# Attention and expert layer on one core: late weight loads moved to the synchronisation engine's queue, zeroing moved to unit 6, one transfer for a unit's maxima, row-max stream one tile further ahead

## The reference

```python
q = (x @ Wq).reshape(B, T, 16, 16).transpose(0, 2, 1, 3)
k, v = ...                                   # 4 key/value heads, each repeated 4 times
att = einsum('bhqd,bhkd->bhqk', q, k) * scale + alibi + causal
att = softmax(att)
y = einsum('bhqk,bhkd->bhqd', att, v) ... @ Wo
x = layernorm(x + y)
logits = x @ router_w.T                      # 8 experts, top 1, sigmoid of the winning logit
routed = sum over experts of (up * silu(gate)) @ down, rows scaled by the score
shared = silu(x @ shared_gate_w) * (x @ shared_up_w) @ shared_down_w
x = layernorm(x + shared + routed)
```

## Time and profile before

| quantity | value |
|---|---|
| median of 3 runs | 568.99 us (565.54 to 570.54) |
| the profiled execution | 567.3 us |
| its span, first to last instruction | 565.6 us |
| PE busy in the span | 511.2 us, 90% |
| ACT, DVE, POOL busy | 260.4, 299.2, 212.4 us |
| mean granted clock of TensorE | 0.951 |

### The profile page before, as it was taken

How to read it: one execution, slowest core, us unless ns; L and a number is a source line. 1 busy time by engine, 2 the same in 40 slices (tenths; PEclk the granted TensorE clock), 3 DMA queues, 4 the chain that set the end, 5 groups by cost and what they waited for, 6 DMA issues and landing times.

```text
span 565.6 us, 7685 instructions
## 1 busy us (share of the span) xinstructions
PE 511.2 (90%) x2474; PEld 250.9 (44%) x2474; DVE 299.2 (53%) x624; ACT 260.4 (46%) x529; POOL 212.4 (38%) x305
## 2 busy tenths in 40 slices
PE   5876799979999999989987989999989999999991
PEld 2322233323332333321245754664665666656561
DVE  1767799978987888880035734212222333323332
ACT  2634487968897879887920031011013222222310
POOL 4433343634443434331201005870003454554543
PEclk9988599999999999998978889999999999999997
DMA  7669420564554545310233700231112222122210
GB/s 219 121 173 301 121 50 3 129 198 92 170 97 164 96 166 114 146 38 3 82 100 115 235 1 1 76 109 39 56 57 66 66 63 77 57 75 67 61 52 28
DMA packets 39462, 54.91 MB, mean 97 GB/s; under 512 B 5887, under 2 KB 27971, under 8 KB 39316
## 3 DMA queue, kind: packets, MB, share of 16 engines
q1 hardware_dynamic: 29792, 30.93, 21.2%
q0 software_dynamic: 5952, 19.56, 11.1%
q10 hardware_dynamic: 3680, 3.94, 2.1%
HBM read 34.72 MB, written 17.52 MB: 92 GB/s over the span
## 4 chain that ended last, share of the span: by engine, by line
PE 71%; DVE 11%; DMA 7%; ACT 4%; issue 3%; SPq 2%; POOL 1%; POOLq 0%; ACTq 0%; DVEq 0%
PE ps L785 14%; PE ps L705 10%; PE ps L607 9%; PE ps L596 7%; PE ps L804 7%; PE ps L583 7%; DVE mx L971 6%; DMA qk_or_dn<-mrow 5%; PE ps L716 5%; PE ps L553 3%; PE ps L677 3%; PE ps L796 2%; ACT probs L886 2%; PE ps L694 1%; DVE eq L966 1%
## 5 line engine op out<-in xcount | busy, mean ns | idle before, releaser
L886 ACT ACTIVATE probs<-ps 128x512 f32<-128x512 f32 x288 | 155.4, 613 | 33.4 <-PE ps L596 33.0
L971 DVE TENSOR_REDUCE mx<-ps 128x1 f32<-128x512 f32 (+3 forms) x240 | 148.2, 649 | 36.2 <-PE ps L583 35.7
L583 PE MATMUL ps<-qk_or_dn 127*128 127x128 bf16 (+3 forms) x576 | 114.4, 284 | 11.9 <-DVE mx L971 6.5
L596 PE MATMUL ps<-qk_or_dn 127*128 127x512 bf16 x288 | 103.6, 392 | 9.0 <-DMA qk_or_dn<-mrow 6.0
L583 PEld LDWEIGHTS ps<-qk_or_dn 127*128 127x128 bf16 x576 | 47.6, 100 | 92.7 <-DVE mx L971 38.4
L785 PE MATMUL ps<-wgu,tmp 128*128 x184 | 82.9, 593 | 0.1
L607 PE MATMUL ps<-probs,Vs 128*32 128x512 f32 x576 | 78.2, 615 | 0.7 <-ACT probs L886 0.7
L1260 POOL TENSOR_SCALAR_AFFINE_SELECT probs<-probs 128x512 f32<-128x512 f32 x64 | 40.7, 636 | 96.1 <-ACT probs L886 96.0
L1219 POOL TENSOR_SCALAR_AFFINE_SELECT dg<-dg 128x512 f32<-128x512 f32 x64 | 40.8, 638 | 46.2 <-ACT dg L842 46.1
L1318 POOL DMA_INDIRECT rows<-acc,tok x23 | 22.6, 981 | 87.7 <-DMA acc<-x_all 42.3
L596 PEld LDWEIGHTS ps<-qk_or_dn 127*128 127x128 bf16 x288 | 26.6, 98 | 55.1 <-ACT probs L886 33.1
(11 more groups left out here) (118 smaller groups left out, 498.3 us busy)
## 6 DMA issues: line engine op xcount, KB each, us to landing
wgu<-in_gu POOLq DMA_DIRECT2D x8, 1024.0 KB, 5.7
qk_or_dn<-qparts SPq DMA_DIRECT2D x36, 128.0 KB
yT<-yU SPq DMA_DIRECT2D x16, 256.0 KB, 2.0
qk_or_dn<-in_dn SPq DMA_DIRECT2D x8, 512.0 KB, 8.2
tmp<-xs SPq DMA_DIRECT2D x23, 128.5 KB, 2.2
qparts<-wgu SPq DMA_DIRECT2D x6, 384.0 KB, 4.1
tmp<-yT SPq DMA_DIRECT2D x34, 64.0 KB
xs<-rows POOLq DMA_DIRECT2D x1, 2056.0 KB, 12.2
```

The lines of the kernel that those rows point to most:

```text
L583: mm = pe.matmul(ps[:, bank, i * w:(i + 1) * w], Q6[k][0:KROWS, h0 + i, qi * P:(qi + 1) * P], K6[k][0:KROWS, k0:k0 + w], start=True, stop= ...
L596: pe.matmul(o, K6[k][0:KROWS, kb * P:(kb + 1) * P], Q6[k][0:KROWS, :, qi * P:(qi + 1) * P], start=True, stop=True).then_inc(s_st, 1)
L886: act.activation(probs[:, 4 * (s % 3) + p, :], ps[:, 4 + (4 * s + p) % SB, :], ACT.Exp, scale=SCALE).then_inc(s_exp, 1)
L971: dve.tensor_reduce(o, ps[:, a_bank(u, t), 0:nh * w].rearrange("p (h w) -> p h w", h=nh), AX.X, ALU.max).then_inc(s_amax, 1)
```

## The change

Four edits. The six late loads leave ACT's projection jobs; SP issues `x_all` at the end of its unit 0 and the five weight loads at the end of its unit 1 (`load_late`), and for this SP's loop is written out. `zero_slots` goes from slot 4 of unit 1 to slot 4 of unit 6. `max_rows` issues one transfer of 3 partitions instead of three of one, and the waits on `s_mrow` count 16 for a unit instead of 48. `AHEAD` goes from 19 to 20 and `FIRST_AHEAD` from 13 to 14.

```diff
-LEAD, AHEAD, FIRST_AHEAD = 6, 19, 13
+LEAD, AHEAD, FIRST_AHEAD = 6, 20, 14
...
                 sp.wait_ge(s_amax, turn_count(u, last))
-                n = HG * NQ
-                for p in range(3):
-                    sp.dma_start(Q6[i][p:p + 1, :, :].rearrange("o h t -> o (h t)")
-                                 .rearrange("o (a b) -> o a b", a=n),
-                                 mrow[p * n:(p + 1) * n, :]).then_inc(s_mrow, 16)
+                sp.dma_start(Q6[i][0:M_ROWS, :, :].rearrange("p h t -> p (h t)")
+                             .rearrange("p (a b) -> p a b", a=HG * NQ), mrow[:]).then_inc(s_mrow, 16)
...
+            def load_late(dst, src, done):
+                sp.dma_start(dst, src.rearrange("(k p) n -> p k n", p=P)).then_inc(done, 16)
...
-            with sp.Fori(0, LOOPS, 1) as it:
-                for k in range(STEP):
-                    step(it * STEP + k, k)
-            for u in range(LOOPS * STEP, NU):
-                step(u, u % STEP, last=(u == NU - 1), more=False)
+            for u in range(NU):
+                step(u, u % STEP, last=u == NU - 1, more=u + 2 < NU)
+                if u == 0:
+                    load_late(x_all[:], x_d, s_x)
+                if u == 1:
+                    for dst, src in ((wo, wo_d), (rt, rt_d)):
+                        load_late(dst[:], src, s_wo)
+                    for dst, src in ((wsg, sg_d), (wsu, su_d), (wsd, sd_d)):
+                        load_late(dst[:], src, s_wsh)
...
-                i = 2 * (n - LATE_AT)
-                for dst, src, done in later_loads[i:i + 2] if i >= 0 else []:
-                    act.dma_start(dst, src.rearrange("(k p) n -> p k n", p=P)).then_inc(done, 16)
...
-                    if s == 4 and u == 1:
+                    if s == 4 and u == NU - 2:
                         zero_slots()
```

More of the change, by code:

```diff
@@ L42 @@
 STEP = 3
-LOOPS = (NU - 2) // STEP
-assert LOOPS * STEP == NU - 2
 CF_ID, CF_SEL, CF_IOTA, CF_LE, CF_THR = 0, 128, 256, 264, 328
@@ L98 @@
 DIRECT = 4
-FIRST_A, LATE_AT, ACT_CASTS = 4, 9, 6
+FIRST_A, ACT_CASTS = 4, 6
 Q_AT, K_AT = (0, (3, 5), 4), (2, (0, 5), 1)
-LEAD, AHEAD, FIRST_AHEAD = 6, 19, 13
+LEAD, AHEAD, FIRST_AHEAD = 6, 20, 14
 BEHIND, ND = 4, 2
@@ L412, in step @@
                 if not last:
-                    max_rows(u + 1, (k + 1) % STEP, isinstance(u, int) and u == NU - 2)
+                    max_rows(u + 1, (k + 1) % STEP, u == NU - 2)
                 store_y(u, 1)
@@ L591, in score @@
                 if s == 0 and p == 0:
-                    pe.wait_ge(s_mrow, u * 48 + 48)
+                    pe.wait_ge(s_mrow, u * 16 + 16)
                     pe.wait_ge(s_vs, u + 1)
@@ L842, in copy_diag @@
                 act.activation(dg[A_TILES[t][0] % ND], ps[:, bank, :], ACT.Copy).then_inc(s_dcopy, 1)
-            later_loads = [(x_all[:], x_d, s_x), (wo[:], wo_d, s_wo), (rt[:], rt_d, s_wo), (wsg[:], sg_d, s_wsh),
-                           (wsu[:], su_d, s_wsh), (wsd[:], sd_d, s_wsh)]
             for n in range(NJ):
@@ L1028, in turned_max @@
                 if u > 0:
-                    dve.wait_ge(s_mrow, u * 48)
+                    dve.wait_ge(s_mrow, u * 16)
                 dve.tensor_copy(mrow[:], ps[0:3 * HG * NQ, a_bank(u, NA - 1), 0:P // 2].bitcast(BF16)
```

## The result

The changed kernel takes 576.36 us (median of 4 runs, 575.06 to 579.9) against 568.51 (4 runs, 565.54 to 570.54) before: ratio **1.0152, 95% interval 1.0087 to 1.0217**. The forecast was 573.6 with a range of 558 to 581, so the time lies inside the range, 2.8 us above the forecast. The profiled execution of the changed kernel is the longest of the four, 579.9 us with a span of 578.2; the spans of the other three are 573.3 to 575.1.

What follows compares the result with a forecast made beforehand. PE bounds it (71% of the chain), stopped by DMA waits in attention units. ACT -1.6, unit 1 +2.7, unit 2 +6.7, units 3 to 5 -2.8, unit 6 -0.4: +4.6 us, median 573.6 us, range 558 to 581.

Steps and rivals of the forecast that it cites:

- Rival (a): Units 1 and 2: the late loads hide, each unit waits only 0.7 us; 559.8 us in all, chance 0.20.
- Part 1, loads off ACT: Projection job 9: ACT no longer held by issuing `wo` behind `x_all`; -1.6 us, bounds 1.0 and 2.1.
- rival (d): Early loads give nothing because the stores of `qparts` set the end there; sum +6.2 us, no chance of its own.
- Part 2 in unit 1: `x_all` ahead of unit 3's load on SP's queue: wait 6.2 us, slow clock 1.4, unit 33.6 us, +2.7.
- Part 2 in unit 2: Five weight loads ahead of the unit's load, plus `wgu` overlap: wait 6.2 us, slow clock 1.4, unit 33.6, +6.7.
- rival (b): Unit 2's load is caught by the `wgu` load if its tail starts after 143 us; 577.6 us, chance 0.20.
- Part 3, stream one place ahead: Loaded unit's first tile and the maxima 0.8 us earlier; load wait 0.7 us per unit in units 3 to 5.
- Part 4, one transfer: Maxima in one transfer land 1.0 us earlier per unit; all waits on maxima in units 1 to 5 go.
- Rival (c): Single maxima transfer slower than the three, on about three engines, four units keep 0.7 us waits; 576.4 us, chance 0.10.
- Part 5, zeroing: Zeroing moved from unit 1 to unit 6: unit 1's 3.1 us wait goes, unit 6 -0.4 us (-1.0 to +1.0).
- The cover I named: Last maxima, colliding with zeroing in unit 6, have some 8 us until unit 7's first score; losing it costs 1 us.
- Long waits: Units 1 and 2: `kparts` waits of 5 to 7 us; forecast fails if ACT and DVE catching up make them cheaper.

Runs made afterwards that it cites:

- e1_late_on_act: Changed kernel with only the six late loads put back on ACT, at projection jobs 9 to 11; 556.87 us, ratio 0.9866 to the kernel before.
- e3_late_on_sp_alone: Kernel before with only the late loads moved to SP, behind units 0 and 1, and SP's loop written out; 574.85 us, ratio 1.0213.
- e12_late_behind_load: Changed kernel with the late loads issued on SP directly behind the unit's load in units 1 and 2, not ahead of it; 564.39 us, ratio 0.9893.
- e9_best_sp: Changed kernel with late loads at the end of SP's unit 5, six `kparts` transfers of 16 rows, second `wgu` load behind slot 8; 555.78 us, ratio 0.9779.
- e7_late_on_sp_unit5: Changed kernel with all six late loads on SP at the end of unit 5, where no unit's load follows; 562.37 us, ratio 0.9901.
- e4_gu_later_unit2: Changed kernel with unit 2's two `wgu` loads issued behind slots 6 and 8 instead of 4 and 6; 569.97 us, ratio 1.0126.
- e6_ahead_alone: Kernel before with only the stream one place ahead (20 and 14); ratio 0.9876 to the kernel before.
- e5_one_transfer_alone: Kernel before with only the single transfer for a unit's maxima; ratio 0.9945 to the kernel before.

## Why the prediction was right, and where its sizes were off

**Sign, mechanism and places** held: two waits of 5 to 8 us on `kparts` in units 1 and 2, all engines idle in their last part, the clock low behind them. `e1_late_on_act` and `e3_late_on_sp_alone` show that the loads on SP's queue make them, and `e12_late_behind_load` that it is their place ahead of the unit's load. Rival (a) falls.

**Part 1, loads off ACT**, -1.6: unit 0 starts at 68.91, was 70.53, so -1.6, but most of that is luck. PE, the changed kernel, then the kernel before:

```profile
43.03 0.46 PE L564 MATMUL ps<-cf,tmp 64*128 64x64 f32 x4 [0.24 <-ACT tmp L862]
...
46.48 0.62 PE L585 MATMUL ps<-qk_or_dn 127*128 127x256 bf16 x6 [2.24 <-ACT dg L844]
...
48.08 1.03 PE L583 MATMUL ps<-qk_or_dn 127*128 127x256 bf16 x6 [0.44 <-ACT dg L842]
```

The gap of 1.75 us is 0.24, as I said. But PE then waits 2.24 us for ACT at the next such place, where it waited 0.44, so that nearly all of it is given back. The rest was there before: the max tiles behind PE's first 2.3 us wait on ACT's diagonal copy start at 30.88 instead of 32.09, 1.2 us earlier, ahead of any late load in either kernel. From there to the tiles at 46.48 and 48.08 it is 15.6 us against 16.0. In this pair the edit shows 0.4 us and not 1.6, below my lower bound of 1.0. Over all kernels the same stretch takes 15.6 to 15.8 us in five and 14.1 in three of the eight with the loads on SP, and 15.9 to 16.5 in five and 14.7 in one of the six with them on ACT, so 0.1 to 0.9 us between like ones. That is nearer to rival (d), in which the early loads give nothing, than to my term.

**Part 2 in unit 1**: 33.6 forecast, 33.8 measured. The groups around the wait, 106.52 and 115.76, are 9.2 us apart, where undisturbed they are 2.9 (`e9_best_sp`). These 6.3 us more are 5.55 of wait, for the 6.2 of the sum, and 0.8 of slow clock in the tiles behind it. The next distance, 4.5 us against 3.1, is the slow clock again, 1.45 us, so 2.2 in all for the 1.4 of the sum. The two errors cancel, and so do two in the wait. Counted from the unit's first `weigh` group, the load lands after 16.6 us in the changed kernel, 11.3 before, and 11.4 in `e7_late_on_sp_unit5`, which has the written-out loop and no backlog. So `x_all` costs 5.2 us where I had 6.3, and the loop, for which I took off 0.9, saves nothing in this unit. That the unit is right to 0.2 us is in part luck.

**Part 2 in unit 2** is the term whose size was off. It had 5.5 for the backlog and the stream, 0.7 for the `wgu` load and 1.4 for the clock; measured are 8.20 for the wait, and for the clock 0.8 in the tiles behind it (152.21 - 140.31 = 11.9 against 2.9, less the wait) and 2.0 in the next group. The 0.7 was taken from the unit where PE stood 0.78 us, a load that a `wgu` transfer just touches at its end. Here the `wgu` load comes 0.35 us behind the last `kparts` issue, at a DMA share of 1.0, and `wsd`, ahead of the whole load, lands only at 144.3; `e4_gu_later_unit2` puts the collision at 3.0 us. That is rival (b), whose condition (the tail of the load starts after 143 us) was met, and whose 577.6 lies 1.2 us above the result, where the forecast lies 2.8 below; it deserved more than 0.20. `e3_late_on_sp_alone`, where the same collision costs about 0.6 us, shows that its size was not to be read from the rows to a microsecond.

**Part 3, stream one place ahead**: taken 0.8 us each way; `e6_ahead_alone` has 0.6 us less on the maxima and 0.5 more on the load for each unit. Units 3 to 5 took 79.9 us, forecast 80.1. Inside that sum two errors cancel. The load's waits of PEld in these units are 15.4 - 5.99 - 8.64 = 0.8 us for all three (the two long ones are those at 114.37 and 150.81 in its timeline), where I took 0.7 each. That the 11 issues take 0.9 us less was right (99.12 to 104.35 in `e7_late_on_sp_unit5`, 5.2 us against 6.1), and in units 3 to 5 it counts in full: the load lands 10.8 to 11.0 us after the unit's first group, 11.6 to 12.3 before. There I should have taken all of it off; `e6_ahead_alone`, which keeps the loop, has 5.0 us of these waits, `e7_late_on_sp_unit5` 1.6. Against this stand the waits on the maxima of the next part.

**Part 4, one transfer**: taken 1.0 us per unit, measured 0.4 alone. "All of them go" failed: 3.5 us of PEld's wait on the maxima remain in four places, up to 1.1, and PE itself stands 0.64 us in one of them, so by my own mark (0.5 us) this part is wrong. All four lie behind the second `wgu` load of the unit, which is issued 0.3 to 0.6 us ahead of the maxima, and with that load behind slot 8 they are gone (`e9_best_sp`). Rival (c), in which the single transfer is slower than three, falls: `e5_one_transfer_alone` has shorter waits than the kernel before. Its 576.4 us is the number nearest to the result, and that is chance.

**Part 5, zeroing**: the 3.1 us of unit 1 went, as expected. Unit 6 has the wrong sign, +0.6 for -0.4: PE waits 3.34 us for the last maxima instead of 2.69.

```profile
262.98 0.31 PE L580 MATMUL ps<-cb,mparts 128*96 128x128 bf16 x1 [3.34 <-DVE mparts L1020]
```

PE waits there for DVE's last maxima, so one tile fewer for PE could not shorten it; I had no ground for a gain from it. What lengthens the wait goes with the zeroing: it is 2.69 to 2.84 us in the four kernels that don't zero in unit 6, one of them with the stream ahead (`e6_ahead_alone`, 2.84), and 3.08 to 3.34 in the ten that do. How the zeroing reaches DVE's maxima was not traced. The cover I named held: in eight of those ten kernels PE doesn't wait on the maxima at unit 7's first score, and in the other two it waits 0.49 and 0.22 us.

**Long waits** were paid in full, and nothing caught up behind them: in the stretches from 111.0 to 114.3 and from 146.0 to 150.5 no engine computed at all. One mark that I named, that `x_all` lands ahead of every part of unit 3, can't be read in full: it lands 9.5 us after its issue, at 107.9, and the last part of the load 6.5 us later, but the rows give no landing for the parts before.

## What to carry to other kernels

In these runs SP's queue made a load wait for what was issued ahead of it (5.55 us), and hardly for the same bytes behind it (1.07 us). So a transfer that nobody needs soon must not stand ahead of one that is needed at once; look at what is issued next on that queue, and at its slack, not at the share of busy DMA engines. A load whose consumer starts in the microsecond in which it lands has no slack: its waits are small today, and what was added ahead of it here was paid in full. Transfers read as 3 and 2 parts showed here as a tail of low DMA share; split so that 16 rows lead, the load took three more issues and was over sooner, though that is worth time only where somebody waits for it. And a start that moves by 4 us between kernels that do the same there can make a term look right: read it at its own place.

## What the runs showed that was not expected

**The clock in unit 6.** The length of unit 6 varies from 26.8 to 29.2 us between the ten kernels that zero there, and not with whether they also have the late loads there (27.9 to 28.9 with, 26.8 to 29.2 without). In all of them PE waits 3.1 to 3.3 us for the last maxima; what differs is mainly the clock behind it. Windows of 4 us behind that wait, of the changed kernel and of `e1_late_on_act`:

```profile
263.00:267.00 4.00, 3.82 (x14) 0.71 (x14) 0.22 (x1) 1.43 (x3) 0.00 (x0) 0.60 1.01 348
```

```profile
247.10:251.10 4.00, 3.74 (x23) 0.85 (x24) 0.22 (x1) 2.66 (x5) 0.64 (x1) 1.00 1.00 344
```

0.60 against 1.00 behind idle times of 3.34 and 3.16 us. In the second, PE did 23 matmuls for 14. In the ten kernels the clock in this window is 0.50 to 0.63, but for this one. The fall of the clock after such a wait is thus not certain, and it is worth about 1.1 us (the group behind is 2.40 us after the one before it instead of 3.49). Which of the two such a wait gets is left open.

**One stall of 3.8 to 4.5 us** stands in the shared expert in the profiled execution of the changed kernel:

```profile
391.52 0.76 DVE L1160 TENSOR_TENSOR x_all<-ps,x_all 128x256 f32<-128x256 f32 x2 [4.53 <-remote]
```

It is not this kernel's own. The same instruction stands 3.8 to 4.5 us, with the same mark, in the profiled executions of all eight kernels of the last two groups of runs (`e5` to `e12`), among them two that are the kernel before with one edit; it is absent in those of the kernel before and of `e1` to `e4`. The trace names no cause for it. It also bears on how far the ratios can be read: they compare whole times, and how many of the other executions have the stall can't be seen. The unit lengths don't contain it, and the readings above rest on them.

**In this backlog both sides paid.** The `wgu` load not only delays the unit's load, it is delayed itself (10.3 us, where the median of the eight is 5.4 to 5.8 in every kernel), and so is `wsd`, 512 KB, which is issued ahead of the unit's load at 133.99 and lands 10.3 us later. Ahead in the queue was dear for those behind, but it did not make these transfers quick.
